# First transfers of a four-layer attention kernel put in another order, with one wait per constant

## What is computed

```python
x = _L0_xattn_ref(ctx_2048, x, mask, ...)      # keys and values: context and x; queries: x; then an MLP
x = _L1_xattn_ref(x, ctx_2048, mask, ...)      # grouped-query attention: 32 query heads, 8 key heads
x = _L2_xattn_ref(x, ctx_2048, 0, ...)         # recurrent layer (RWKV form) with token shift and a scan
x = _L3_xattn_ref(x, ctx_2048, mask, ...)      # attention on the normalised context, tanh(gate) * out

# of layer 0
q = (latents @ q_w + q_b).reshape(b, k_len, NH, DH)
kv = (h @ kv_w + kv_b).reshape(b, p + k_len, NH, DH, 2)     # h = concat([context, x], axis=1)
attn = softmax(where(full_mask, einsum('bkhd,bnhd->bhkn', q, kmat) / DH, -inf))
```

## Time and profile before

| | us |
|---|---|
| median of the runs | 1259.38 |
| lowest and highest of three runs | 1259.19, 1260.45 |
| profiled execution, its own time | 1264.44 |
| span of the profiled execution | 1262.5 |
| PE busy | 1127.0 (89% of the span) |
| DVE busy | 956.6 (76%) |
| ACT busy | 651.5 (52%) |
| POOL busy | 261.0 (21%) |

### The profile page before, as it was taken

One profiled execution on the slowest core, in us unless ns is written; L12 is line 12 of the kernel. 1 busy time (PEld: TensorE's weight loads), 2 busy tenths in 40 slices (PEclk: granted clock), 3 DMA queues, 4 the chain that ended last, 5 costly groups with the idle time before them and its releaser, 6 DMA issues. The chain is left out here.

```text
span 1262.5 us, 24184 instructions
## 1 busy us (share of the span) xinstructions
PE 1127.0 (89%) x7776; PEld 765.1 (61%) x7776; DVE 956.6 (76%) x3401; ACT 651.5 (52%) x2483; POOL 261.0 (21%) x349
## 2 busy tenths in 40 slices
PE   5878899999999998999999998999999998897656
PEld 4564666665665666666666666666666666554434
DVE  2707697789967998789968998689968998675834
ACT  1528343784448553774448553674438553582024
POOL 3210223102410214102420214102321214101310
PEclk9788899999999999999999999999999999898858
DMA  8000000000000000000000000000000000000000
GB/s 296 2 9 20 1 2 1 22 2 15 2 21 2 16 1 1 22 2 16 1 22 2 12 5 1 22 2 15 1 22 2 6 11 1 1 2 11 1 1 9
DMA packets 18092, 18.91 MB, mean 15 GB/s; under 512 B 7216, under 2 KB 16432, under 8 KB 17712
## 3 DMA queue, kind: packets, MB, share of 16 engines
q1 hardware_dynamic: 17968, 17.37, 4.6%
HBM read 15.27 MB, written 2.10 MB: 14 GB/s over the span
## 5 line engine op out<-in xcount | busy, mean ns | idle before, releaser
L831 ACT ACTIVATE E<-S,nmax 128x128 f32<-128x128 f32 (+1 forms) x1024 | 424.1, 416 | 229.4 <-DVE nmax L1020 215.1
L1020 DVE CUSTOM_DVE_ANT_0 S<-psS,mb 128x128 f32<-128x128 f32 (+1 forms) x1024 | 264.3, 320 | 87.7 <-PE psS L534 64.4
L494 PE MATMUL ring<-slot,w_l 128*128 128x256 f32 x992 | 251.5, 400 | 14.0 <-DVE slot L1202 5.2
L494 PEld LDWEIGHTS ring<-slot,w_l 128*128 128x128 f32 x992 | 188.8, 198 | 60.0 <-issue 12.8
L548 PEld LDWEIGHTS psT<-ident,E 128*128 128x128 f32 x1280 | 146.2, 147 | 128.1 <-ACT E L831 73.3
L534 PE MATMUL psS<-keys,slot 32*128 32x512 f32 (+1 forms) x768 | 194.4, 581 | 30.1 <-DVE nmax L1020 19.0
L1035 DVE COPY ET<-psT 128x512 f32<-128x512 f32 x320 | 206.2, 681 | 7.8 <-PE psT L548 7.8
L548 PE MATMUL psT<-ident,E 128*128 128x128 f32 x1280 | 203.8, 293 | 7.8 <-DVE ET L1035 3.2
L831 ACT ACTIVATION_READ_ACCUMULATOR E<-S,nmax 128x1 f32 x1024 | 191.6, 187 | 0.0
L504 PE MATMUL ring<-w_l,slot 128*128 128x256 f32 (+1 forms) x640 | 151.9, 384 | 7.7 <-DVE slot L1051 5.8
L504 PEld LDWEIGHTS ring<-w_l,slot 128*128 128x128 f32 x640 | 115.3, 194 | 36.6 <-issue 10.7
(11 more groups left out here) (119 smaller groups left out, 1183.3 us busy)
## 6 DMA issues: line engine op xcount, KB each, us to landing
slot<-in_ctx SPq DMA_DIRECT2D x8, 256.0 KB, 2.7
slot<-in_x SPq DMA_DIRECT2D x8, 256.0 KB, 2.7
w_l<-in_wl SPq DMA_DIRECT2D x1, 2048.0 KB, 11.2
out<-slot SPq DMA_DIRECT2D x8, 256.0 KB, 2.1
w_l<-in_wl SPq DMA_DIRECT2D x2, 768.0 KB, 7.1
w_l<-in_wl SPq DMA_DIRECT2D x1, 1152.0 KB, 9.9
m0i<-in_m SPq DMA_DIRECT2D x8, 128.0 KB, 3.2
mb<-in_m SPq DMA_DIRECT2D x8, 128.0 KB, 2.8
```

Of the source, the lines that this page charges most:

```text
L494: m = pe.matmul(b[:, a, :], w[:, k, m0 + a * P:m0 + (a + 1) * P], src[:, k, :], start=(k == 0), stop=(k == kt - 1))
L831: ins = act.activation(E[:, g % RING_E, h * w:(h + 1) * w], S[:, g % RING_S, h * w:(h + 1) * w], ACT.Exp, bias=nmax[:, g % 4, h:h + 1], sc ...
L1020: ins = dve.tensor_tensor_reduce(S[:, g % RING_S, h * w:(h + 1) * w], psS[g % 2][:, h * w:(h + 1) * w], bias[:, bb, :], -1.0, HUGE, ALU.ad ...
```

## The change

It does four things. (1) SP issues `program("start")` first, so context, x and mask lead; the constants follow, W0's q, k and v parts in three transfers of 256 KB with a semaphore each, the gate before the k part, the first row of biases (v0_b) before W1 and the other six rows after it. (2) PE begins when `ident` stands (s_const at 2); it waits for a weight part at q0, k0c, k0l, v0c and v0l, and for DVE's set-up at the first job. (3) ACT and DVE wait for column constants and gate alone (`SMALL_IN`); DVE waits for the zeros and the rows where it first uses them, at v0c, v0l and v1. (4) POOL fills gather_j first, signals s_const after the two small constants, and fills V0, wP, V1 and V3 behind that; it waits for the rows too before its program.

```diff
-WEIGHTS_IN = 4 * 16
+SMALL_IN = 2 * 16
...
+        s_wq, s_wk, s_wv = (sem(f"weights0_{n}_in") for n in "qkv")
+        s_row, s_rows, s_zeros = sem("first_row_in"), sem("rows_in"), sem("zeros")
...
         @block.sync
         def _(sp):
-            sp.dma_start(W0t[:, 0:qkv], wl0[:, 0:qkv]).then_inc(s_w, 16)
-            sp.dma_start(colt[:, :, :], cols).then_inc(s_w, 16)
-            sp.dma_start(rowt[:, :, :], rows.partition_broadcast(P)).then_inc(s_w, 16)
-            sp.dma_start(gate_t[:, 0:1], gate.partition_broadcast(P)).then_inc(s_w, 16)
...
             program("start", None)
+            sp.dma_start(W0t[:, 0:CT * C], wl0[:, 0:CT * C]).then_inc(s_wq, 16)
+            sp.dma_start(colt[:, :, :], cols).then_inc(s_w, 16)
+            sp.dma_start(gate_t[:, 0:1], gate.partition_broadcast(P)).then_inc(s_w, 16)
+            sp.dma_start(W0t[:, CT * C:2 * CT * C], wl0[:, CT * C:2 * CT * C]).then_inc(s_wk, 16)
+            sp.dma_start(W0t[:, 2 * CT * C:qkv], wl0[:, 2 * CT * C:qkv]).then_inc(s_wv, 16)
+            sp.dma_start(rowt[:, 0:1, :], rows[:, 0:1, :].partition_broadcast(P)).then_inc(s_row, 16)
             sp.dma_start(W1t[:, :], wl1).then_inc(s_w1, 16)
+            sp.dma_start(rowt[:, 1:, :], rows[:, 1:, :].partition_broadcast(P)).then_inc(s_rows, 16)
             by_column_tile(W0t, wl0, qkv, s_w0)
...
         @block.tensor
         def _(pe):
-            pe.wait_ge(s_setup_d, 4)
-            pe.wait_ge(s_w, WEIGHTS_IN)
+            pe.wait_ge(s_const, 2)
...
                         if layer == 0:
+                            if phase == "first":
+                                pe.wait_ge(s_setup_d, 4)
...
                     elif step == "q0":
                         pe.wait_ge(leaves("xT"), left("xT"))
+                        if phase == "start":
+                            pe.wait_ge(s_wq, 16)
...
         @block.scalar
         def _(act):
-            act.wait_ge(s_w, WEIGHTS_IN)
+            act.wait_ge(s_w, SMALL_IN)
...
-            dve.wait_ge(s_w, WEIGHTS_IN)
-            dve.wait_ge(s_setup, 1)
+            dve.wait_ge(s_w, SMALL_IN)
...
                     elif step == "v0c":
+                        if phase == "start":
+                            dve.wait_ge(s_zeros, 1)
+                            dve.wait_ge(s_row, 16)
...
                     elif step == "v1":
+                        if phase == "start":
+                            dve.wait_ge(s_zeros, 1)
+                            dve.wait_ge(s_rows, 16)
+                            dve.wait_ge(s_setup, 1)
...
+            pool.memset(gather_j[:, :, :], 0.0)
             pool.memset(ident[:, :], 0.0).then_inc(s_const, 1)
...
-            for buf in (gather_j, V0, V1, V3, wP):
-                shape = buf.shape
-                pool.memset(buf[tuple(slice(None) for _ in shape)], 0.0)
             pool.memset(minus_half[:, :], -0.5)
             pool.memset(eps_g[:, :], 1e-5).then_inc(s_const, 1)
-            pool.wait_ge(s_w, WEIGHTS_IN)
+            for buf in (V0, wP, V1, V3):
+                shape = buf.shape
+                ins = pool.memset(buf[tuple(slice(None) for _ in shape)], 0.0)
+            ins.then_inc(s_zeros, 1)
+            pool.wait_ge(s_w, SMALL_IN)
+            pool.wait_ge(s_rows, 16)
             pool.wait_ge(s_setup_d, 4)
```

More of the change, by code:

```diff
@@ L643, in program @@
                         pe.wait_ge(leaves("cT"), left("cT"))
+                        if phase == "start":
+                            pe.wait_ge(s_wk, 16)
                         channel_major("k0c", W0["k"], cT)
                     elif step == "k0l":
+                        if phase == "start":
+                            pe.wait_ge(s_wk, 16)
                         channel_major("k0l", W0["k"], xT)
                     elif step == "v0c":
+                        if phase == "start":
+                            pe.wait_ge(s_wv, 16)
                         token_major("v0c", cT, W0["v"])
                     elif step == "v0l":
+                        if phase == "start":
+                            pe.wait_ge(s_wv, 16)
                         token_major("v0l", xT, W0["v"])
```

## The result

The changed kernel takes **1264.0 us** (median of 20 runs, 1261.9 to 1269.1); the kernel before took 1259.8 us beside it (20 runs). The ratio is **1.0033, 95% interval 1.0017 to 1.0049**: slower by a third of a per cent, 4.2 us, where the forecast was 1259.8 us and no difference. The profiled execution took 1263.31 us.

What follows compares the result with a forecast made beforehand. It took POOL's lane copies and keys, waiting for the staged v and g transfers, to bound the first scores. Entry's 4.7 us covered (0), queue 0, clock +0.4 on 1259.38 us gave 1259.8 us; range 1256.8 to 1262.4 us.

Steps and rivals of the forecast that it cites:

- The chain that decides: Start of the first scores: transfer queue, POOL's lane copies, then masked keys decide; the entry is ready 0.5 to 2 us earlier.
- The entry, term by term: PE's products before the first scores: q0 4.7 us earlier, at 8.1 instead of 12.86 us, all hidden behind POOL.
- Waits added at nothing: New waits for zeros, six rows and DVE's set-up before the first scores: all met in time, costing nothing.
- The transfer queue … I take 0: Landing of layer 2's v and g weights: queue limited by its bytes, so 0 us, with -1.5 and +1.5 kept.
- upper bound of 1.5 us: Latest v and g landing allowed: three more issues at 0.50 us each, if place in the queue counted.
- The rule weighed: Skill's DMA advice to coalesce, at least 1 MiB per transfer: splitting 768 KB in three would be a loss; set aside.
- The case's row of a lone transfer: A lone 256 KB transfer lands in 2.7 us, 0.67 us of it bytes, leaving a fixed 2.0 us.
- The row of x: x landed only 0.7 us behind the context, read as fixed 2.0 us costs overlapping in a full queue.
- The clock, +0.4 us: PE's longer idle time drops its clock before the first scores: four score matmuls take 2.08 instead of 1.68 us.
- The rivals on the clock: Clock rises one pair of jobs later (1262.0 us, chance 0.13) or earlier (1257.6 us, chance 0.10), 2.2 us each.
- Sum: Whole kernel: entry's gain covered 0, queue 0, clock +0.4, giving 1264.8 us profiled and 1259.8 us median.
- The one rival with this sign and nearly this size: Each transfer pays its fixed 2.0 us in the queue: v and g 6.1 us later, 1265.5 us; chance 0.03.

Runs made afterwards that it cites:

- a_copies_mid: Changed kernel with POOL's eight lane copies moved from ahead of the first masked keys into the first phase's step of the transposes nT; 1253.1 us, ratio 0.9933.
- a_vg_first: Changed kernel with layer 2's two staged v and g transfers issued right behind the rows, ahead of W0's pieces; 1251.8 us, ratio 0.9938.
- controls: Second profiled executions, one each of the unedited kernels before and after the change, on one chip; 1259.09 us (before) and 1262.09 us (after).
- a_unsplit: Changed kernel with W0's q, k and v parts joined in one transfer and all seven rows in one, between gate and W1; 1262.8 us, ratio 1.0026.
- a_head_whole: Changed kernel with W0's entry weights as one 768 KB transfer at the head, ahead of context, tokens and mask; 1264.6 us, ratio 1.0027.
- a_w_first: Changed kernel with its three 256 KB entry weight pieces issued ahead of context, tokens and mask; 1267.6 us, ratio 1.0037.
- b_start_first: Kernel before with context, tokens and mask issued ahead of its four whole constants, waits as before; 1261.2 us, ratio 1.0018.
- b_copies_mid: Kernel before with POOL's eight lane copies moved into the first phase's step of the transposes nT; 1255.6 us, ratio 0.9951.
- b_ctx_second: Kernel before with context and tokens issued behind the whole entry weights and ahead of columns, rows and gate; 1257.8 us, ratio 0.9980.

## Why the prediction was wrong, point by point

- **The chain that decides: right.** Queue, lane copies, keys, scores; a_copies_mid and a_vg_first show it: with the copies moved the first scores wait for DVE's last values at 21.1 us, and with the transfers moved they come at 21.7 us, 0.6 us behind that.
- **The entry, term by term: right.** The forecast was q0 at 8.1 us behind ACT's tanh; it was 7.63. The gate was expected at 7.3 us and landed at 3.17 + 3.7 = 6.9. The entry's end was forecast at 21.8 us and came at 19.96 (the first 28 matmuls took 7.99 us instead of 9.27 us). All of it was hidden by POOL, as said.
- **Waits added at nothing: right.** No row names one of the new semaphores as what ended an idle time on the way to the scores. One cover shrank: DVE's set-up took 6 us (from 1.97 to 8.0) where it had taken 2.6 us, more than the twice that I allowed, and the cT copy behind it ran at 7.95 us. No row names it as what ended a wait: PE works on without one from 7.63 us.
- **"The transfer queue … I take 0": the step that failed.** The measured term is +3.7 us (24.60 to 28.27 us) in the profiles shown and +3.1 us in the controls, more than twice the upper bound of 1.5 us. The reasoning was "limited by its bytes", read from a DMA share of 0.98. The runs showed in its place that the same bytes take longer: 272 instead of 392 GB/s at 3 to 6.75 us and 266 GB/s at 20 to 24 us, where the same window of the control moves 394, at shares of 0.94 and 0.98. In the kernels of before that differ in the order of the transfers alone the queue ran between 285 and 319 GB/s up to 20 us, at the same bytes; with the changed kernels it is 264 to 319 GB/s. The upper bound came from the issue rate only and never asked what a queue slower than 357 GB/s would do. The issue was indeed 3.4 us late, but a_unsplit has it on time and the landing still late, so the place in the queue isn't what counted. Why the order slows the engines stays open.
- **The rule weighed: neither it nor my row was right.** The Trainium skill (DMA: Bandwidth & Descriptors, Rules for kernel authors) asks to coalesce. The case's row of a lone transfer priced three more of them at 2.0 us each, 6.1 us. The sign was right and the measured whole was 3.1 to 3.7 us; but joining the pieces left the lane copies 0.5 us earlier than in one profile of the change and 0.5 us later than in the other (a_unsplit), and made them 0.9 us earlier in a_head_whole against a_w_first, within the 1.0 us by which two profiles of one kernel differ. So most of the loss isn't shown to be a cost per transfer, and b_start_first, with no more transfers than before, has most of it. The row of x, from which I had excluded such a cost, stood in a queue in its good order.
- **The clock, +0.4 us: right.** It had fallen before the first scores, and the first group took 2.08 us; from the first scores to the second it is 3.75 us instead of 3.35. Against the control of before (1.13 us) it was 0.95 us. The rivals on the clock named something real: whole pairs of jobs at the low clock do come and go, between executions of one kernel (the two profiles of before) and between kernels (a_copies_mid and b_copies_mid). In the change itself the fifth group is at the high clock, as in the control of before.
- **Sum.** With +3.6 us for the first scores, 1259.8 becomes 1263.4 us; 1264.0 was measured. The fit within 0.6 us is partly luck, since one pair of jobs at the low clock is worth 2.2 us. The one rival with this sign and nearly this size had 0.03, and the range ended 1.6 us below.

## What to carry to other kernels

An early chain that isn't the last one gives nothing back, and the transfers that it needs early are taken from the chain that is: ask which consumer waits for the *end* of the queue, and move its data or its work first (here v and g, or POOL's copies: 0.6 to 0.9% faster with the same early entry). Don't read a busy DMA share as a limit by bytes: compare the GB/s at the same share, and don't carry a rate that one order of transfers shows over to another (272 and 266 GB/s here, where before and its control moved 392 and 394 in the same windows). When one profile of each kernel disagrees with the medians, take profiles whose own times lie near the medians before explaining a span, and look for rows of the same work at two clocks.

## What was not expected of the hardware

- The rate of one queue differs with the order of its first transfers: 285 to 319 GB/s over the first 20 us with the same bytes and nothing else changed, where three profiles of one order are 298 to 311 GB/s. The landing marks of one transfer are between 0.5 us (b_ctx_second) and 4.5 us (b_start_first) apart. What sets the engines apart stays open: neither the mask's place, nor the gate's, nor the pieces, nor a long transfer at the head explains it alone.
- SP issues more slowly beside the slow queue: it took 5.81 us for the first eight pieces of W0 (4.18 us before) and 4.24 us for those of W3 (3.68 us before), and v and g are issued 3.4 us later. That the queue holds its issuer is argued, not shown; and the late issue isn't what makes the landing late (a_unsplit).
- DVE's copies beside POOL's large fills ran far longer. Before, behind the fills, and after, beside them (the last row is the end of POOL's fills after):

```profile
7.98 0.22 DVE L964 COPY ones<-head 128x128 f32<-128x128 f32 x1
8.12 1.17 DVE L968 COPY spread<-ident 128x128 f32<-128x128 f32 x8
```
```profile
3.12 3.74 DVE L978 COPY ones<-head 128x128 f32<-128x128 f32 x1
3.26 4.61 DVE L982 COPY spread<-ident 128x128 f32<-128x128 f32 x8
```
```profile
4.08 2.70 POOL L1342 MEMSET V<- 128x2048 f32 x2
```

The same copy took 0.22 us and 3.74 us. POOL's fills end at 6.78 us, that copy at 6.86 us and the other eight by 7.87 us. The copy began beside the first fill, which ended at 3.67 us, and it ended only behind the last one. No row shows a wait for them here.
